# Product-key experts of a fused multi-layer kernel: 16-bit one-hot operands in SBUF, value parts on VectorE, weighting on GpSimd, one-hot chunks taken in pairs

## The reference, cut to what matters

```python
xn = _rmsnorm(_layernorm(h), norm_w)
q = (xn @ w_q.T).reshape(b, t, 8, 2, 128)
sim1 = jnp.einsum('bthd,hkd->bthk', q[..., 0, :], keys[:, :, 0, :])     # 64 keys
sim2 = jnp.einsum('bthd,hkd->bthk', q[..., 1, :], keys[:, :, 1, :])
s1, i1 = jax.lax.top_k(sim1, 8)
s2, i2 = jax.lax.top_k(sim2, 8)
all_idx = (i1[..., :, None] * 64 + i2[..., None, :]).reshape(b, t, 8, 64)
all_sc = (s1[..., :, None] + s2[..., None, :]).reshape(b, t, 8, 64)
fs, pk = jax.lax.top_k(all_sc, 8)
fi = jnp.take_along_axis(all_idx, pk, axis=-1)                          # 64 experts a token
hidden = jax.nn.gelu(jnp.einsum('btd,bthkd->bthk', xn, expert_down[fi]), approximate=False)
hidden = hidden * jax.nn.relu(fs)
return jnp.einsum('bthk,bthkd->btd', hidden, expert_up[fi])
```

## Time and profile before

| what | value |
|---|---|
| median of 3 runs | 5288.62 us (5287.6 to 5290.49) |
| profiled execution, its own time | 5291.85 us |
| its span | 5290.1 us |
| TensorE busy in the span | 4550.0 us (86%) |
| VectorE busy | 3673.4 us (69%) |
| ScalarE busy | 2155.6 us (41%) |
| GpSimd busy | 2512.1 us (47%) |
| product-key layer | from about 4047 us to the end |
| chain that ended last | GpSimd L3134 8% of the span, TensorE L3059 7%, L2957 2%, L2990 1% |

### The profile page before, as it was taken

One profiled execution on the slowest core, in us unless ns is written; L12 is line 12 of the kernel. 1 busy time (PEld: TensorE's weight loads), 2 busy tenths in 40 slices (PEclk: granted clock), 3 DMA queues, 4 the chain that ended last, 5 costly groups with the idle time before them and its releaser, 6 DMA issues. The chain is left out here.

```text
span 5290.1 us, 65217 instructions
## 1 busy us (share of the span) xinstructions
PE 4550.0 (86%) x22312; PEld 2893.2 (55%) x22312; DVE 3673.4 (69%) x7355; ACT 2155.6 (41%) x4039; POOL 2512.1 (47%) x1494
## 2 busy tenths in 40 slices
PE   7888599768888888888886999896998899999999
PEld 4555267533333333333332446793445788888888
DVE  4764222258989888998987223214885999999997
ACT  3654011135555555555554223234663232233322
POOL 3441400269999999999996000000221443334333
PEclk8998799879989999999988999897998899999999
DMA  1003123322222222222221000570002000000000
GB/s 71 1 1 111 59 69 121 114 69 68 68 70 70 70 68 71 68 70 69 70 67 59 0 6 1 224 283 29 1 0 84 3 5 5 5 3 5 5 5 5
DMA packets 153112, 287.22 MB, mean 54 GB/s; under 512 B 24441, under 2 KB 135024, under 8 KB 144206
## 3 DMA queue, kind: packets, MB, share of 16 engines
q1 hardware_dynamic: 144926, 263.59, 15.1%
q0 software_dynamic: 6656, 14.04, 0.9%
q10 hardware_dynamic: 1200, 5.42, 0.3%
HBM read 252.33 MB, written 33.42 MB: 54 GB/s over the span
## 5 line engine op out<-in xcount | busy, mean ns | idle before, releaser
L1509 PE MATMUL ssm_ps<-ssm_hc,net_ident 128*128 128x452 f32 x2048 | 959.0, 595 | 193.0 <-DVE ssm_hc L1765 106.6
L1691 POOL TENSOR_TENSOR ssm_dBu<-ssm_du,ssm_bc 128x904 f32<-128x904 f32 x512 | 1066.9, 2109 | 3.2 <-POOL ssm_du L1709 1.7
L1610 ACT ACTIVATE ssm_ps<-ssm_step,ssm_decay 128x448 f32<-128x448 f32 x1024 | 647.6, 636 | 646.4 <-DVE ssm_ps L1755 435.5
L1509 PEld LDWEIGHTS ssm_ps<-ssm_hc,net_ident 128*128 128x128 f32 x2048 | 391.6, 204 | 727.8 <-issue 347.8
L1755 DVE TENSOR_TENSOR_SCAN ssm_ps<-ssm_ps,ssm_dBu 128x452 f32<-128x452 f32 x512 | 565.1, 1104 | 131.9 <-POOL ssm_dBu L1691 45.6
L1755 DVE TENSOR_TENSOR_SCAN ssm_hs<-ssm_ps,ssm_dBu 128x452 f32<-128x452 f32 x512 | 551.3, 1077 | 41.4 <-ACT ssm_ps L1610 36.9
L1702 POOL TENSOR_TENSOR ssm_hc<-ssm_hs,ssm_bc 128x904 f32<-128x904 f32 x256 | 539.6, 2108 | 74.4 <-DVE ssm_hs L1755 74.2
L3134 POOL TENSOR_TENSOR peer_hot_parts<-peer_hot_cols,peer_parts 128x1024 bf16<-128x1024 bf16 (+1 forms) x240 | 433.8, 1810 | 127.1 <-DVE peer_hot_cols L3152 114.2
L2990 PE MATMUL peer_ps<-peer_xn,peer_down 128*128 128x226 f32 x2048 | 447.7, 365 | 0.0
L3059 PE MATMUL peer_ps<-peer_hid,peer_up 128*128 128x226 f32 x2048 | 398.2, 354 | 1.6 <-DVE peer_hid L3186 1.6
L3059 PEld LDWEIGHTS peer_ps<-peer_hid,peer_up 128*128 128x128 f32 x2048 | 388.9, 190 | 6.5 <-issue 2.2
(11 more groups left out here) (424 smaller groups left out, 8047.7 us busy)
## 6 DMA issues: line engine op xcount, KB each, us to landing
ssm_bc<-ssm_rows SPq DMA_DIRECT2D x256, 452.0 KB, 3.6
ex_w<-in_l_ffn_w SPq DMA_DIRECT2D x64, 1024.0 KB, 6.6
moe_w_gu<-in_moe_gate_up SPq DMA_DIRECT2D x16, 704.0 KB
slots_in<-rt_zeros SPq DMA_DIRECT2D x17, 640.0 KB, 8.6
moe_rows_in<-slots_in SPq DMA_DIRECT2D x16, 512.0 KB
slots_out<-xp_rows_out SPq DMA_DIRECT2D x16, 512.0 KB
moe_w_dn<-in_moe_down SPq DMA_DIRECT2D x16, 384.0 KB
peer_down<-in_peer_down_t SPq DMA_DIRECT2D x1, 4096.0 KB, 16.5
```

What stands on the lines that cost most here:

```text
L1509: nc.tensor.matmul(Y_BANK[j][:, 0:GT], c["ident"][:, :], hc[:, q % 2, j, :], start=False, stop=(n == S - 1))\
L1610: nc.scalar.activation(rows(dA(i % 2))[:, :, lo:lo + N - 1], rows(step[hf.d][:, j, :])[:, :, lo:lo + N - 1], ACT.Exp, scale=decay[hf.d][:, ...
L1691: nc.gpsimd.tensor_tensor(dBu[:, q % 2, j:j + 2, :], du[hf.d][:, j:j + 2, :], bc[:, q % RING, 0:1, :].to_broadcast([P, 2, GT]), ALU.mult). ...
```

## The change

Four things, all in `peer`:

1. **16-bit one-hot operands.** ScalarE copies the two code rows from PSUM to SBUF as bf16, each value written twice in a row (`codes16`), and a bf16 ramp is made once (`ramp16`). The comparisons read and write bf16 in SBUF with pairs as the innermost dimension.
2. **Parts on VectorE.** The three parts of a chunk are written by one VectorE operation of 8x3x64 elements (`weighted`), from `hot_cols` and pairs of `parts`. GpSimd writes no `hot_parts` any more, LEAD goes, and VectorE runs `compared(ch + 1)` ahead of `weighted(ch)`. `hot_cols` has two buffers, and a comparison waits for the `weighted` of two chunks earlier. GpSimd still splits the score once a step, now into pairs.
3. **Weighting on GpSimd.** The 16 multiplications of `hid` by `weight` move from VectorE to GpSimd, behind the same two waits. The norm's scaling on VectorE moves in between the two sequences of `best_experts`.
4. **Order.** On TensorE and ScalarE the codes are transposed and copied ahead of `hidden(0)` of the step. Chunk 0 comes after `hidden(3)`, then two chunks after every second call: 1 and 2 after `hidden(5)`, and so on to 11 and 12 after `hidden(15)`; 13 and 14 follow as before.

```diff
-parts = st.sbuf("parts", [P, 3, N], BF16)
...
+parts = st.sbuf("parts", [P, N, 3, 2], BF16)
+codes16 = st.sbuf("codes16", [P, 2, N, 2], BF16)
+ramp16 = st.sbuf("ramp16", [P, P], BF16)
...
-hot_cols = st.sbuf("hot_cols", [P, HB, CHUNK, PB * EB], BF16)
-hot_parts = st.sbuf("hot_parts", [P, HB, 3, CHUNK, PB * EB], BF16)
+hot_cols = st.sbuf("hot_cols", [P, 2, CHUNK, PB * EB], BF16)
+hot_parts = st.sbuf("hot_parts", [P, HB, CHUNK, 3, PB * EB], BF16)
...
-def best_experts(dve, k):
+def best_experts(dve, k, normed):
...
     for b in range(PB):
+        if b and normed is not None:
+            norm.vector_scale(nc, dve, normed)
...
+def chunks_behind(i):
+    if i < LAG or (i - LAG) % 2:
+        return ()
+    return (0,) if i == LAG else (i - LAG - 1, i - LAG)
...
-                pe.wait_ge(s["lead_done"], at + 1)
...
-                                              hot_parts[:, at % HB, i, t, :], start=(i == 0), stop=(i == 2))
+                                              hot_parts[:, at % HB, t, i, :], start=(i == 0), stop=(i == 2))
...
             for k in range(len(backs)):
+                if k:
+                    codes_turned(pe, k)
                 for i in range(HU if k else 0):
                     hidden(k, i)
-                    if i == 1:
-                        codes_turned(pe, k)
-                    if 0 <= i - LAG < NC:
-                        weights(k, i - LAG)
+                    for ch in chunks_behind(i):
+                        weights(k, ch)
...
+                nc.scalar.activation(codes16[:, :, :, :].rearrange("p a n d -> p (a n) d"),
+                                     ps[7][:, 0:2 * N].unsqueeze(2).to_broadcast([P, 2 * N, 2]), ACT.Copy).then_inc(s["ct_done"], 1)
+                nc.scalar.activation(parts[:, :, 0, :], ps[7][:, 2 * N:3 * N].unsqueeze(2).to_broadcast([P, N, 2]), ACT.Copy)\
+                    .then_inc(s["ct_done"], 1)
...
-                act.wait_ge(s["ct_done"], 3 * k + 1)
-                nc.scalar.activation(LEAD, parts[:, 0, :], ACT.Copy).then_inc(s["ct_done"], 1)
...
             for k in range(len(backs)):
-                pool.wait_ge(s["ct_done"], 3 * k + 2)
+                pool.wait_ge(s["ct_done"], 3 * k + 3)
...
-                for ch, (t0, n) in enumerate(CHUNKS):
-                    at = k * NC + ch
-                    pool.wait_ge(s["hot_done"], at + 1)
-                    if at >= HB:
-                        pool.wait_ge(s["g_mm"], at - HB + 1)
-                    nc.gpsimd.tensor_tensor(hot_parts[:, at % HB, 1:3, 0:n, :],
-                                            hot_cols[:, at % HB, 0:n, :].unsqueeze(1).to_broadcast([P, 2, n, PB * EB]),
-                                            parts[:, 1:3, t0:t0 + n].unsqueeze(3).to_broadcast([P, 2, n, PB * EB]), ALU.mult)\
-                        .then_inc(s["cols_done"], 1)
+                nc.gpsimd.tensor_tensor(parts[:, :, 2, :], rest[:, :].unsqueeze(2).to_broadcast([P, N, 2]), parts[:, :, 1, :],
+                                        ALU.subtract).then_inc(s["part_done"], 1)
+                pool.wait_ge(s["gelu_done"], (k + 1) * HU)
+                pool.wait_ge(s["evac_done"], (k + 1) * NC)
+                for i in range(HU):
+                    block_ = hid[:, i * J:(i + 1) * J, :]
+                    nc.gpsimd.tensor_tensor(block_, block_, weight[:, i * J:(i + 1) * J, :, :].rearrange("p j b n -> p j (b n)"),
+                                            ALU.mult).then_inc(s["wgt_done"], 1)
...
-            def one_hot(k, ch):
+            def compared(k, ch):
...
-                    dve.wait_ge(s["ct_done"], 3 * k + 3)
+                    dve.wait_ge(s["ct_done"], 3 * k + 1)
                 if at >= HB:
                     dve.wait_ge(s["g_mm"], at - HB + 1)
-                    dve.wait_ge(s["cols_done"], at - HB + 1)
...
+                if at >= 2:
+                    dve.wait_ge(s["cols_done"], at - 1)
+                for i, (hot, width, done) in enumerate(((hot_rows[:, at % HB], P, "rows_done"), (hot_cols[:, at % 2], PB * EB, "hot_done"))):
+                    shape = [P, n, width // 2, 2]
+                    nc.vector.tensor_tensor(hot[:, 0:n, :].rearrange("p t (e d) -> p t e d", d=2),
+                                            ramp16[:, 0:width].rearrange("p (e d) -> p e d", d=2).unsqueeze(1).to_broadcast(shape),
+                                            codes16[:, i, t0:t0 + n, :].unsqueeze(2).to_broadcast(shape), ALU.is_equal)\
+                        .then_inc(s[done], 1)
+
+            def weighted(k, ch):
+                t0, n = CHUNKS[ch]
+                at = k * NC + ch
+                shape = [P, n, 3, PB * EB // 2, 2]
                 dve.wait_ge(s["hot_done"], at + 1)
...
+                if ch == 0:
+                    dve.wait_ge(s["ct_done"], 3 * k + 2)
+                    dve.wait_ge(s["part_done"], 2 * k + 2)
+                nc.vector.tensor_tensor(hot_parts[:, at % HB, 0:n, :, :].rearrange("p t i (e d) -> p t i e d", d=2),
+                                        hot_cols[:, at % 2, 0:n, :].rearrange("p t (e d) -> p t e d", d=2).unsqueeze(2)
+                                        .to_broadcast(shape), parts[:, t0:t0 + n, :, :].unsqueeze(3).to_broadcast(shape), ALU.mult)\
+                    .then_inc(s["cols_done"], 1)
...
+            nc.vector.tensor_copy(ramp16[:, :], ramp[:, :]).then_inc(s["ramp_done"], 1)
+            best_experts(dve, 0, None)
...
             for k, back in enumerate(backs):
+                compared(k, 0)
                 for ch in range(NC):
-                    one_hot(k, ch)
+                    if ch + 1 < NC:
+                        compared(k, ch + 1)
+                    weighted(k, ch)
                 if fronts[k] is not None:
                     dve.wait_ge(s["hid_mm"], (k + 1) * HU)
                     scaled_input(dve, k + 2)
                 if afters[k] is not None:
...
-                dve.wait_ge(s["gelu_done"], (k + 1) * HU)
-                dve.wait_ge(s["evac_done"], (k + 1) * NC)
-                for i in range(HU):
-                    block_ = hid[:, i * J:(i + 1) * J, :]
-                    nc.vector.tensor_tensor(block_, block_, weight[:, i * J:(i + 1) * J, :, :].rearrange("p j b n -> p j (b n)"),
-                                            ALU.mult).then_inc(s["wgt_done"], 1)
-                if afters[k] is not None:
-                    norm.vector_scale(nc, dve, k + 3)
                 if fronts[k] is not None:
-                    best_experts(dve, k + 1)
+                    best_experts(dve, k + 1, k + 3 if afters[k] is not None else None)
```

More of the change, by code:

```diff
@@ L2823, in peer @@
                  "split_done", "hit_done", "mul_done", "sel_done", "u_done", "bits_done", "code_done", "t_done", "ct_done",
-                 "hid_mm", "gelu_done", "rows_done", "hot_done", "lead_done", "rest_done", "part_done", "cols_done", "g_mm", "evac_done", "wgt_done", "up_mm", "res_done")
+                 "hid_mm", "gelu_done", "ramp_done", "rows_done", "hot_done", "rest_done", "part_done", "cols_done", "g_mm", "evac_done", "wgt_done", "up_mm", "res_done")
         s = {x: st.sem(x) for x in names}
@@ L3069, in turned_codes @@
                         if k:
-                            act.wait_ge(s["lead_done"], k * NC)
                             act.wait_ge(s["cols_done"], k * NC)
-                        nc.scalar.activation(parts[:, 0, :], ps[7][:, 2 * N:3 * N], ACT.Copy).then_inc(s["ct_done"], 1)
+                        nc.scalar.activation(codes16[:, :, :, :].rearrange("p a n d -> p (a n) d"),
+                                             ps[7][:, 0:2 * N].unsqueeze(2).to_broadcast([P, 2 * N, 2]), ACT.Copy).then_inc(s["ct_done"], 1)
+                        nc.scalar.activation(parts[:, :, 0, :], ps[7][:, 2 * N:3 * N].unsqueeze(2).to_broadcast([P, N, 2]), ACT.Copy)\
+                            .then_inc(s["ct_done"], 1)
                         nc.scalar.activation(value[:, :], ps[7][:, 2 * N:3 * N], ACT.Copy).then_inc(s["ct_done"], 1)
-                        act.wait_ge(s["ct_done"], 3 * k + 1)
-                        nc.scalar.activation(LEAD, parts[:, 0, :], ACT.Copy).then_inc(s["ct_done"], 1)
                     def evacuate(k, ch):
@@ L3100, in _ @@
                     for k in range(len(backs)):
+                        if k:
+                            turned_codes(k)
                         for i in range(HU if k else 0):
                             gelu(k, i)
[L3103 to L3106, removed]
+                            for ch in chunks_behind(i):
+                                evacuate(k, ch)
                         for ch in range(HU - LAG if k else 0, NC):
@@ L3119, in _ @@
                     for k in range(len(backs)):
-                        pool.wait_ge(s["ct_done"], 3 * k + 2)
+                        pool.wait_ge(s["ct_done"], 3 * k + 3)
                         if k:
                             pool.wait_ge(s["cols_done"], k * NC)
```

(29 more changed lines are left out.)

2 lines of the change are left out of this document (removed).

## The result

The changed kernel takes **5209.68 us** (median of 4 runs, 5201.97 to 5212.38) against 5289.56 for the kernel before, a ratio of 0.9847 (95% interval 0.983 to 0.9864). The forecast was 5210. The profiled execution took 5212.38 us, 79.5 less than that of before.

What follows compares the result with a forecast made beforehand. VectorE's 2.45 us a chunk was taken as the bound. Removing 5.05 us in each of 15 steps, plus 7 in the first, less 0.2 and 4.4, gave 78 us less: 5210 us, range 5191 to 5262.

Steps and rivals of the forecast that it cites:

- What bounded the kernel: In the one-hot chunks, VectorE sets the pace at 2.45 us a chunk; TensorE needs 2.23 us.
- Durations at half pace: VectorE's all-16-bit SBUF operations take half of 0.53 us per 512 elements, plus 0.15 us fixed; a chunk costs 1.93 us.
- slack of 0.36 us: In chunk pairs, VectorE's margin before TensorE wants chunk 6; no wait between chunks while a VectorE chunk stays under 2.1 us.
- Per step: Gain in each step: 6.35 us of TensorE idle time less 1.0 and 0.3 us charged, so 5.05 us.
- Chunk 13: Ahead of chunk 13, TensorE still waits for its late weighting: 1.0 us a step charged in place of 1.75.
- all 6.35 us: TensorE's idle time in a 74.95 us step: 2.0 us before chunk 0, 2.6 between chunks, 1.75 before chunk 13.
- Codes first: At the start of a step, codes are ready before the earlier transposes; the 2.0 us wait ahead of chunk 0 goes.
- First and last step: First step's chunks 7 us shorter, ramp copy costs 0.2; last step 4.4 us longer, without similarities to cover GpSimd's weighting.
- Sum: Whole kernel: 15 steps of 5.05 us, plus 7, less 0.2 and 4.4, make 78 us less, median 5210.
- A: Up product waits for GpSimd's weighting above 1.20 us a block; 5256 us at 1.4; chance 0.07 mild, 0.04 beyond 1.53.
- B: On VectorE, the parts operation stays at full pace: a chunk of 2.72 us, 5301 us in all; chance 0.07.
- C: On VectorE, 16-bit operands change nothing: 3.51 us a chunk, 11 us more a step, about 5477 us; chance 0.05.

## Why the prediction was right, point by point

- **What bounded the kernel**: right. VectorE's 2.45 us a chunk was the pace; at 2.00 the waits go but for chunk 13's, at 2.80 (f32 ramp) they grow.
- **Durations at half pace**: 0.68, 0.42 and 0.95 us were forecast (0.60, 0.34 and 0.99 from start to start), 0.69, 0.42 and 0.95 came. A chunk is 2.00 us and not 1.93, because the comparison behind a weighting starts 0.11 us after its end. The slack of 0.36 us took it.
- **Per step**: 5.03 us against 5.05, out of errors that cancel. Chunk 13 costs 0.64 us, 1.0 was charged. GpSimd costs nothing, 0.3 was charged. Against that, the sum counted all 6.35 us as idle time to be had, but the six pairs of `hidden` calls that follow bf16 matmuls each cost 0.08 us more than the 3.06 it works with; 0.2 is left over.
- **Codes first**: no wait, but with less to spare. The codes are ready at 4646.70 for transposes at 4649.25, 2.5 us ahead and not 3.8: `pair` and the norm's scaling beside GpSimd and the waits for similarities took the rest. I charged the contention to GpSimd alone; both bear it. VectorE's first `pair` takes 0.80 us more and its norm scaling 0.45. On GpSimd the two blocks that meet them take 1.59 and 1.54 us, 0.85 more in all; it comes out even because the others start every 1.10 us and not every 1.14, so the 16 take 18.46.
- **First and last step**: the mean that ends the first step's chunks starts at 4125.87, 6.9 us earlier (7 forecast). The last step is 3.9 us longer (4.4): from the start of the weighting to the end 30.9 us, 27.0 before.
- **Sum**: 15 x 5.03 + 6.9 - 3.9 = 78.5 of 79.5 measured between the two profiled executions. Most of the missing 1.0 is a term that the prediction does not have: behind the chunks of the first step the granted clock was 0.81 in the kernel before (4132 to 4140) and 0.99 now (4125 to 4133), and the mean took 1.67 us there, 0.85 now.
- **The parts of the change**: the prediction treated them as four edits, the runs show that they are not separable. Order alone 0, everything but the move of the parts +80 us, everything but the weighting's move -27 of -80 us. Pairs against single chunks bring nothing; their place in the prediction, with a slack of 0.36 us, was not needed.
- **Rivals**: A stands near (0.5 to 0.7 us of room) and did not happen. B and C did not; the f32-ramp kernel, with a chunk of 2.80 us, shows about what B's 2.72 would have cost, 5320 and not 5301. C's 3.51 no run shows. One figure beside the sum is off: 5211 for blocks of 1.22 us leaves out the 1.3 us of hold-ups that the sum itself has; with them it is 5230.

## What to carry to other kernels

A VectorE operation with two inputs ran at twice the pace here when all its operands were 16-bit, and lost it with one in f32; a broadcast operand can be made to fit by writing each value twice. The same step puts both its inputs in SBUF, where it and GpSimd's operations wait for each other; so take GpSimd's work away from beside it, and give it other work for a stretch in which VectorE reads PSUM. Price a wait of TensorE at more than its length when its clock may fall behind it.

## What the runs showed that was not expected

- VectorE's `tensor_tensor` with both inputs in SBUF does not run beside a GpSimd `tensor_tensor`: 0.69 us became 2.18 beside one of 2.02; with one operand in PSUM 1.21 stayed 1.21 beside 1.90. The Trainium skill names contention at an SBUF interface shared by the two engines, when VectorE has two SBUF inputs (GPSIMD Engine Reference, Specifications); the traces agree. I had priced it at 0.3 us a step.
- A single call of `hidden` between bf16 matmuls takes 1.61 us and not 1.53.
- The same idle time of TensorE, 2.58 us, was followed by a granted clock of 0.80 in 9 of 14 steps and by 1.00 in 5; in the order-alone kernel it fell in 3 of 14. What decides it stays open.
